# A fused hybrid network on one core: rotary split, forget-gate store and weight loads moved between stages

## The reference

```python
x = x + _L0_attn_a_ref(_layernorm(x), ...)   # selective scan (state space), 16 states
x = x + _L0_ffn_ref(_layernorm(x), ...)      # fp4 block-quantised gated FFN
x = x + _L0_attn_b_ref(_layernorm(x), ...)   # masked linear attention, rows normalised
x = x + _L0_ffn_ref(_layernorm(x), ...)
x = x + _L1_attn_a_ref(_layernorm(x), ...)   # forgetting attention, 16 heads of 64
x = x + _L1_ffn_ref(_layernorm(x), ...)      # x @ sign(weight)
x = x + _L1_attn_b_ref(_layernorm(x), ...)   # rotary attention, 16 heads of 8
x = x + _L1_ffn_ref(_layernorm(x), ...)
```

## Time and profile before

| | us |
|---|---|
| median of 3 runs | 2292.94 (2290.7 to 2298.5) |
| profiled execution, its own time | 2297.52 |
| its span, first to last instruction | 2295.7 |
| PE busy | 1917.0 (84%) |
| DVE busy | 1503.1 (65%) |
| ACT busy | 1379.4 (60%) |
| POOL busy | 1001.4 (44%) |

### The profile page before, as it was taken

How to read it: one execution, slowest core, us unless ns; L and a number is a source line. 1 busy time by engine, 2 the same in 40 slices (tenths; PEclk the granted TensorE clock), 3 DMA queues, 4 the chain that set the end, 5 groups by cost and what they waited for, 6 DMA issues and landing times. The chain is left out here.

```text
span 2295.7 us, 36184 instructions
## 1 busy us (share of the span) xinstructions
PE 1917.0 (84%) x11875; PEld 885.0 (39%) x11875; DVE 1503.1 (65%) x2277; ACT 1379.4 (60%) x2289; POOL 1001.4 (44%) x1110
## 2 busy tenths in 40 slices
PE   5468885677968748999999999999999767699997
PEld 2123333444654313444444444444444323222222
DVE  5979995793359667787777787777786437311112
ACT  3557773343344336766776667677665435699994
POOL 0167771560136314656666656566656622300001
PEclk9779998798979869999999999999999979799998
DMA  2000000000000011111111112111111101321210
GB/s 91 0 14 0 0 0 1 0 1 1 0 0 1 0 54 47 51 55 51 55 58 58 55 56 57 50 58 59 58 54 63 38 10 37 101 55 46 52 42 37
DMA packets 71431, 84.47 MB, mean 37 GB/s; under 512 B 20544, under 2 KB 44032, under 8 KB 71168
## 3 DMA queue, kind: packets, MB, share of 16 engines
q1 hardware_dynamic: 66224, 79.80, 11.7%
q10 hardware_dynamic: 5040, 2.56, 0.4%
HBM read 71.95 MB, written 9.57 MB: 36 GB/s over the span
## 5 line engine op out<-in xcount | busy, mean ns | idle before, releaser
L1692 DVE SCALAR_TENSOR_TENSOR fu_kv<-fu_ps_kv,fa_vec,fu_kv 128x511 f32<-128x511 f32 x366 | 252.8, 740 | 6.2 <-ACT fu_kv L1622 5.2
L2089 ACT ACTIVATE rt_p<-rt_ps_s 128x1024 f32<-128x1024 f32 x256 | 240.4, 1042 | 26.2 <-PE rt_ps_o L2034 17.4
L1773 POOL TENSOR_TENSOR fu_p<-fu_p 128x768 f32<-128x768 f32 x64 | 116.8, 1824 | 289.2 <-PE fu_ps_n L1467 284.1
L1437 PE MATMUL fu_ps_s<-fu_qn,fu_kn 64*128 64x512 f32 (+3 forms) x1024 | 190.0, 468 | 12.8 <-DVE fu_sg L1738 6.9
L1672 DVE TENSOR_REDUCE fu_nm<-fu_ps_m 128x2 f32<-128x1024 f32 x64 | 78.4, 1225 | 164.9 <-PE fu_ps_m L1460 164.9
L623 POOL TENSOR_TENSOR scan_hC<-scan_h,scan_c 128x1024 f32<-128x1024 f32 x64 | 150.9, 2357 | 71.5 <-DVE scan_h L599 71.5
L1467 PE MATMUL fu_ps_n<-fu_p,fu_vt 128*64 128x512 f32 (+3 forms) x1024 | 166.1, 445 | 0.0
L599 DVE TENSOR_TENSOR_SCAN scan_h<-scan_dA,scan_ps_b 128x1024 f32<-128x1024 f32 x64 | 146.4, 2287 | 2.2
L522 PE MATMUL scan_ps_y<-scan_hC,w_ident 128*128 128x512 f32 x256 | 125.2, 611 | 27.0 <-POOL scan_hC L623 15.4
L2034 PE MATMUL rt_ps_o<-rt_p,rt_va 128*32 128x512 f32 x1024 | 138.1, 611 | 10.0 <-ACT rt_p L2089 8.1
L1495 PE MATMUL fu_ps_kv<-w_XN,fa_wp 128*128 128x512 f32 x244 | 125.7, 639 | 17.6 <-DVE fu_cr L1665 15.4
(11 more groups left out here) (364 smaller groups left out, 5096.0 us busy)
## 6 DMA issues: line engine op xcount, KB each, us to landing
fu_rb<-rms_rows SPq DMA_DIRECT2D x256, 128.0 KB, 2.9
fu_ro<-rms_rows SPq DMA_DIRECT2D x128, 128.0 KB, 2.9
ra_stackq<-rope_parts SPq DMA_DIRECT2D x168, 32.0 KB
ra_stackk<-rope_parts SPq DMA_DIRECT2D x168, 32.0 KB
w_X<-in_xT SPq DMA_DIRECT2D x4, 512.0 KB
fa_wp<-in_wp SPq DMA_DIRECT2D x8, 256.0 KB
fu_cr<-ncum_rows SPq DMA_DIRECT2D x128, 3.0 KB
rope_parts<-rp_hi SPq DMA_DIRECT2D x16, 128.0 KB, 2.4
```

Of the source, the lines that this page charges most:

```text
L1437: pe.matmul(sps[:, h, at:at + T - t * P], k[head(h), t * P:(t + 1) * P], q[head(h), t * P:T], start=(at == 0), stop=False)
L1692: dve.scalar_tensor_tensor(acc, projected(a, k)[:, 0:T - j], vec[:, a % GA, at:at + 1], acc, ALU.mult, ALU.add).then_inc(done, 1)
L1773: pool.tensor_tensor(tail, tail, P13[:, :, 0:3 * P], ALU.add).then_inc(s.d1, 1)
L2089: act.activation(pr[k % 2][i][:, :, :], sps[(U * n + u) % RING][:, :, :], ACT.Exp, scale=DH_B ** -0.5).then_inc(s.exp, 1)
```

## The change

Three parts. (1) SP issues the 23 later loads after `X`, before its waits; ACT issues the 12 early ones only. (2) `CR`, `MHL` and `NC` belong to the outer stage `fa`; DVE's memsets stand in stage `fg` behind `ones`; SP issues the store of `NC` there without waiting, and in `fu` SP alone waits for its landing; PE and SP no longer wait for memsets. (3) The split of batches 6 and 7 (`LATE = 2`) moves from stage `rp` to `rt`: `un`, `HI`, `MID`, `LO` belong to the outer stage `ra`. In `rt` DVE rounds `HI` and `MID` (not ACT), POOL takes the rests between its copies for batch 0 and batch 1, and SP issues the 12 stores before its loads for batch 1.

```diff
@@ -267,6 +268,8 @@
...
                     sp.dma_start(X[:, b:b + 2, :], w.xT_dram[:, b:b + 2, :]).then_inc(s.x, 16)
+                for src, dst in w.loads:
+                    sp.dma_start(dst, src).then_inc(w.loaded, 16)
                 sp.wait_ge(s.load, 16 * 5)
@@ -336,8 +339,6 @@
...
                     act.dma_start(dst, src).then_inc(w.early, 16)
-                for src, dst in w.loads:
-                    act.dma_start(dst, src).then_inc(w.loaded, 16)
                 act.wait_ge(w.early, 16 * w.early_count)
@@ -1223,8 +1224,10 @@
...
     with Stage(nc, "fa") as outer:
+        loaded, stored = outer.sems("loaded stored")
         held = named(
-            wp=outer.sb("wp", [P, GA, 4, P]), wo=outer.sb("wo", [P, GA, P]), vec=outer.sb("vec", [P, GA, 3 + 2 * TAPS]), loaded=outer.sems("loaded").loaded,
+            wp=outer.sb("wp", [P, GA, 4, P]), wo=outer.sb("wo", [P, GA, P]), vec=outer.sb("vec", [P, GA, 3 + 2 * TAPS]), nc=outer.sb("nc", [P, KF, T], BF16), cr=[outer.sb(f"cr{k}", [P, T], BF16) for k in range(3)], mhl=outer.sb("mhl", [P, NT, 2, DH_A], BF16),
+            loaded=loaded, stored=stored,
         )
@@ -1248,8 +1251,7 @@
...
                 sp.wait_ge(s.lo, 1)
-                sp.dma_start(ncum_rows, NC[:, :, :]).then_inc(s.put, 16)
-                sp.wait_ge(s.put, 16)
+                sp.dma_start(ncum_rows, NC[:, :, :]).then_inc(held.stored, 16)
             @block.tensor
@@ -1271,6 +1273,14 @@
...
                 dve.memset(ones[:, :], 1.0).then_inc(s.ones, 1)
+                for k in range(3):
+                    dve.memset(CR[k][:, :], 0.0).then_inc(s.zero, 1)
+                dve.memset(MHL[:, :, :, :], 0.0).then_inc(s.zero, 1)
+                dve.wait_ge(s.zero, 4)
+                for h in range(2):
+                    for k in range(3):
+                        dve.memset(CR[k][64 * h:64 * h + 5, :], 1.0).then_inc(s.made, 1)
+                dve.memset(MHL[:, :, :, 0:3], 1.0).then_inc(s.made, 1)
                 dve.wait_ge(s.ones, 1)
@@ -1382,8 +1391,7 @@
...
                 sp.wait_ge(held.loaded, 16 * (GA + 2))
-                sp.wait_ge(s.set, 9)
-                sp.wait_ge(s.ones, 6)
+                sp.wait_ge(held.stored, 16)
                 for i in range(-AHEAD, U + OUT + 2):
@@ -1655,14 +1661,6 @@
...
             def _(dve):
-                for k in range(3):
-                    dve.memset(CR[k][:, :], 0.0).then_inc(s.set, 1)
-                dve.memset(MHL[:, :, :, :], 0.0).then_inc(s.set, 1)
-                dve.wait_ge(s.set, 4)
-                dve.memset(MHL[:, :, :, 0:3], 1.0).then_inc(s.set, 1)
-                for h in range(2):
-                    for k in range(3):
-                        dve.memset(CR[k][64 * h:64 * h + 5, :], 1.0).then_inc(s.ones, 1)
                 dve.wait_ge(held.loaded, 16 * (GA + 2))
@@ -1821,9 +1817,11 @@
...
         stack = [outer.sb(f"stack{n}", [64 + ROPE_ROWS, HEADS_B // 2, T], BF16) for n in "qk"]
+        parts = [outer.sb(n, [P, 2, B, T], BF16) for n in ("hi", "mid", "lo")]
+        un = [outer.sb(f"un{k}", [P, 2, T]) for k in range(2)]
         first = outer.sems("first").first
-        rope_project(nc, w, XN, V, parts_dram, stack, first)
-        rope_attend(nc, w, X, V, parts_dram, stack, first)
+        rope_project(nc, w, XN, V, parts_dram, stack, first, parts, un)
+        rope_attend(nc, w, X, V, parts_dram, stack, first, parts, un)
 def load_stack(sp, stack, parts_dram, n, pairs, sem):
@@ -1864,9 +1863,9 @@
...
                 load_stack(sp, stack, parts_dram, 0, slice(0, HEADS_B // 2), first)
-                for n in range(2, B):
+                for n in range(2, SPLIT):
                     put(n, s.put)
-                sp.wait_ge(s.put, 16 * 6 * (B - 1))
+                sp.wait_ge(s.put, 16 * 6 * (SPLIT - 1))
                 sp.wait_ge(first, LOAD_FIRST)
@@ -1931,7 +1930,7 @@
...
                         act.activation(sq[:, :, :], rot[last % 2][:, :, :], ACT.Square).then_inc(s.sq, 1)
-                    if real(older):
+                    if 0 <= older < SPLIT:
                         act.wait_ge(s.un, older + 1)
@@ -1943,21 +1942,21 @@
...
                         act.activation(V[:, n, :], sums[:, 0, :], ACT.Copy).then_inc(s.vc, 1)
-                    if real(older):
+                    if 0 <= older < SPLIT:
                         act.wait_ge(s.d1, older + 1)
...
             def _(pool):
-                for n in range(B):
+                for n in range(SPLIT):
                     pool.wait_ge(s.hi, n + 1)
...
                     pool.tensor_tensor(LO[:, :, n, :], d1[n % 2][:, :, :], MID[:, :, n, :], ALU.subtract).then_inc(s.lo, 1)
-                pool.wait_ge(s.lo, B)
-
-
-def rope_attend(nc, w, X, V, parts_dram, stack, first):
+                pool.wait_ge(s.lo, SPLIT)
+
+
+def rope_attend(nc, w, X, V, parts_dram, stack, first, parts, un):
     ROWS = ROPE_ROWS
@@ -1977,7 +1976,10 @@
...
         tps = fps[:, :].rearrange("p (t a b) -> p t a b", t=NT, a=4)
-        s = st.sems("ones low high va sc exp pv osb t ri ot t2 otc f x")
+        HI, MID, LO = parts
+        rest = [st.sb(f"rest{k}", [P, 2, T]) for k in range(LATE)]
+        late = range(B - LATE, B)
+        s = st.sems("hi rest mid lo put ones low high va sc exp pv osb t ri ot t2 otc f x")
         def batches(step):
@@ -1989,8 +1991,17 @@
...
                 def step(n, last):
-                    if n is None or n == 0:
+                    if n is None:
                         return
+                    if n == 0:
+                        for k, m in enumerate(late):
+                            for part, (done, tile) in enumerate(((s.hi, HI), (s.mid, MID), (s.lo, LO))):
+                                sp.wait_ge(done, k + 1)
+                                for j in range(2):
+                                    sp.dma_start(parts_dram[part, j, :, m, :], tile[:, j, m, :]).then_inc(s.put, 16)
+                        return
+                    if n == late[0]:
+                        sp.wait_ge(s.put, 16 * 6 * LATE)
                     for half in range(2):
@@ -2009,7 +2020,15 @@
...
                         pool.tensor_copy(va[:, t, :, 0:DH_B], src).then_inc(s.va, 1)
+                    if i == 0:
+                        for k, m in enumerate(late):
+                            pool.wait_ge(s.hi, k + 1)
+                            pool.tensor_tensor(rest[k][:, :, :], un[m % 2][:, :, :], HI[:, :, m, :], ALU.subtract).then_inc(s.rest, 1)
+                        for k, m in enumerate(late):
+                            pool.wait_ge(s.mid, k + 1)
+                            pool.tensor_tensor(LO[:, :, m, :], rest[k][:, :, :], MID[:, :, m, :], ALU.subtract).then_inc(s.lo, 1)
                 pool.wait_ge(s.va, NT * B)
+                pool.wait_ge(s.lo, LATE)
             @block.tensor
@@ -2092,6 +2111,12 @@
...
             def _(dve):
+                for m in late:
+                    dve.tensor_copy(HI[:, :, m, :], un[m % 2][:, :, :]).then_inc(s.hi, 1)
+                for k, m in enumerate(late):
+                    dve.wait_ge(s.rest, k + 1)
+                    dve.tensor_copy(MID[:, :, m, :], rest[k][:, :, :]).then_inc(s.mid, 1)
+
                 def take(m, q4):
```

25 lines of the change are left out of this document (11 added, 14 removed).

## The result

The changed kernel takes **2272.7 us** (median of 4 runs, 2268.2 to 2275.1) against 2293.5 (4 runs, 2290.7 to 2298.5) for the kernel before on the same chip: ratio 0.9905, 95% interval 0.9881 to 0.9929. The forecast of 2275.2 is a ratio of 0.9923 and lies inside the interval. The profiled execution took 2275.1 with a span of 2273.2, 22.5 less than the span before.

The account below looks back on a forecast made before the run. TensorE was busiest at 84%, but the edit touches three seams where every engine waits for the slowest. Terms -1.7 - 6.8 - 9.2 = -17.7 us took the median from 2292.94 to 2275.2, range 2268.5 to 2282.5.

Parts of the forecast that it names:

- seam 1: Weights stage to first layernorm: moving the later loads to SP lets TensorE start earlier, -1.6 to -1.8 us, taken -1.7.
- seam 2: Gates to forgetting attention: the store's landing wait and the memsets leave the path, -6.6 to -6.9 us, taken -6.8.
- seam 3: Rotary projection to attention: the stage ends at the last `un`; -8.3 to -9.9 us with interference, taken -9.2.
- its chain gets nothing new: Weights stage: VectorE's work gets no new waits, so its old end at 18.67 us ends the stage.
- The sign of being right, 19.5 to 19.8: TensorE's first layernorm matmul was to start at 19.5 to 19.8 us, with ScalarE's last activation ahead of 17.
- bare seam: Time from a stage's last instruction to TensorE's first of the next, priced at 0.83 to 1.08 us.
- Interference: Start of rotary attention: VectorE's roundings and GpSimd's values tile exclude each other, delaying the values pass 0 to 1.35 us, taken 0.5.
- The covers: Rotary attention: moved roundings and stores finish before VectorE's first output copy and SP's batch 1 loads, each covered by 3 us.
- A stall of SP's queue: Rival in the weights stage: SP issues loads at 1.3 us each, not 0.50, losing that gain or more; chance 0.11.
- The seams shrank: Answers the rival that stage ends wait for something unseen, such as outstanding transfers: about -13.5 us, 2279.4; chance 0.05.
- Clock sooner: Rival at the first layernorm: TensorE's shorter pause brings its fast clock back earlier, at most to 2273 us; chance 0.05.
- The slower case: Rival in rotary attention: TensorE's clock rises much later than 9 us behind the seam, 2303 us at 32 steps; chance 0.02.

Follow-up runs that it names:

- the second: The changed kernel timed again with no edit against the kernel before: 2273.5 us against 2295.3, ratio 0.9915.
- second profile of before: The kernel before, unchanged, run and profiled again: 2298.6 us against 2296.1, ratio 1.0007.

## Why the prediction was right

**The sum.** Forecast -17.7; the local readings are -1.7 to -1.8 for seam 1 (means over profiles), -6.64 for seam 2, -9.80 for seam 3 and 0.4 to 0.6 given back behind it, together -17.5 to -17.8. The measured difference of the medians was -20.8 the first time and -21.8 the second; the ratio's intervals reach from -14 to -27 us, so the 3 to 4 beyond the forecast are not established by the times. In the profiles something of that size is there, in TensorE's clock in the last stage: 3.6 in the first pair and 2.8 against the second profile of before. The sum had no term for it.

**Seam 1** was right in its result and wrong in its working; that the result fits is luck. The step "its chain gets nothing new" failed: VectorE's chain waits for TensorE's products of the early weights, and those landed 1.3 to 2.3 later than the 13.66 on which the step rested. "I take 0.50 each" held for the later loads (0.43 to 0.67) but not for the first, 1.72, nor for ScalarE's issues beside it, 1.45. Against that stood a start that was early by chance: the 21.33 of the profile shown is the earliest of the five in which ScalarE issues the later loads, with no long issue in it. The two misses, about 0.8 each on average, cancel. The sign of being right, 19.5 to 19.8, was missed by 0.9; ScalarE's end ahead of 17 came. A sign of being wrong did come: SP had issue rows over 0.6 in the first 20 us (1.72, 0.63, 0.67 and 0.65). SP's issues ended at 18.43 instead of 16.8, still ahead of VectorE, so this cost nothing by itself.

**Seam 2** was right term by term: the landing 2.0, the memsets 4.79 (4.8 at most had been said), the slip on the chain 0.08 (0.1 to 0.3), TensorE 6.64 closer (6.6 to 6.9). The bare seam of 1.15 lies just outside the 0.83 to 1.08. The weights, taken as landed in good time, were in by less than a microsecond, as the share of 0.19 up to 816.5 shows.

**Seam 3** was right: 0.91 from the last `un` to the first score (0.8 to 1.1), 9.80 gained (9.6 to 9.9), the values pass at 3.77 (3.2 to 4.5). Interference was taken at 0.5 between 0 and 1.35, and is 0.59. The order differed from both ends of that range. The forecast had roundings get in ahead of GpSimd, up to two of them in full length, or GpSimd always first at no cost. In fact GpSimd's memset came first and the first rounding waited for it; that rounding's end and the second rounding then held one copy each, by 0.34 and 0.45. The covers held. The last rounding ended 8.95 behind the first score (about 8 had been said), and the four took 6.2 and not 3.4 at most, since they and GpSimd's subtractions held each other up too. The output copy still waited for TensorE, and SP's stack loads came at 15.9.

**The rivals.** A stall of SP's queue as a rate did not come: all 23 issues had ended at 18.43. A milder form did, through the early loads, which landed later. The seams shrank. "Clock sooner" is not shown. From the start of the first layernorm to the scan it took 23.2 in the first profile of before and 22.1 in that of the changed kernel, but 21.6 in the second profile of before, so the difference is one between executions. The slower case did not occur: in the rotary attention the values passes ran at 1.06 from 1981.33 on, 8.8 behind the first score, as before.

## What to carry to other kernels

At a seam, read who ended last and what each engine waited for just before; the work to move is what lies behind the last thing that must be there, and it needs a place where its engine is idle and whose users come late. When an issue of transfers is moved to another queue, ask which transfers it will now run beside, not only whose instruction stream it leaves. A term of one or two microseconds that is read from a single execution is no firmer than that stage's own variation: here a second profile of the same kernel moved the first seam by 1.3 us.
